# Output projection, layer normalisation and gate logits merged into one stage, with the gate weights stationary in four column groups and one softmax over all tokens

## The chip, the cores and the metric

The kernel is one program on one core of a Trainium2 chip. The metric is the device time of one execution in microseconds (us). The core has five engines that run their own queues and meet only through semaphores: TensorE (PE), VectorE (DVE), ScalarE (ACT), GpSimd (POOL) and SyncE (SP); transfers are issued from the queues of SP, ACT and POOL.

## The reference

The whole function is two transformer-like layers on x of 8 x 1024 x 256 in float32: attention, a routed mixture of experts, a phase attention and a soft mixture of experts, each on a normalised input. The change concerns this part of the first layer:

```python
# end of the attention: ctx is 8 x 1024 x 256
x  = x + ctx @ Wo + bo
xn = (x - mean(x)) / sqrt(var(x) + 1e-5)           # over the 256 features
logits   = einsum('bsd,de->bse', xn, gate_w)       # 8 experts
affinity = softmax(logits, axis=-1)
gating, index = top_k(transpose(affinity), 256)    # per batch and expert, of 1024 tokens
```

The chosen rows of xn then go through their expert, are weighted by gating, and are added to x.

## The kernel before

The program is a row of stages. Each stage (class Stage) has its own tiles and semaphores, begins with a barrier of all engines, and hands its results to the next stage through device memory (DRAM). A token tile is 128 tokens in 128 partitions; there are 64 of them. Three stages and a search stand between the attention (attend) and the experts:

- **project** (pj_ names): 16 turns of four token tiles (512 tokens). SP loads the attention's output, already transposed (ctxT, tile pj_c), and the residual x (tile pj_x), four turns ahead. POOL adds the bias to x (L866), PE multiplies ctx with Wo (L842: per turn four tiles by two halves of the 256 features), DVE adds the two (L859), and ACT's queue stores x1 (L850). No engine waits in one turn for another turn's tail, except through the four buffers.
- **normalise** (n_ names, called three more times elsewhere): eight turns of 1024 tokens. DVE takes mean and variance (L149, L154), ACT the square root (L199), DVE reciprocal, scales (L166, L167) and the normalised xn (L175), PE transposes it (L191), ACT copies that out of PSUM (L217), and ACT's queue stores xn (L211) and xnT (L222).
- **route** (rt_ names): eight turns of one batch. SP loads xnT, PE multiplies with the tokens as the weights and the 256 x 8 gate matrix as the moving operand (L942), DVE and ACT compute a softmax per batch (L967 to L974, exponential L959). Then PE turns the affinities so that each of 128 partitions holds 512 tokens of one batch and expert (L947), and DVE searches: 32 rounds of max, max_index and match_replace (L990 to L992), after which the sorted halves are merged and the weights and indices stored.

An engine executes its instructions strictly in the order in which they are written; a wait blocks all that is behind it on that engine.

Of the kernel before, what the change touches and what calls it, by code (L numbers as in the profile page):

```python
# [9 lines left out]
ALU = mybir.AluOpType  # L10
# [3 lines left out]
P = 128  # L14
# [777 lines left out]
def project(nc, tag, ctxT_d, w_d, b_d, x_d, out_d):  # L792

    TC = 4
    TURNS = TILES // TC
    N = TC * P
    U = 4
    rows = lambda d, t: d[t * N:(t + 1) * N, :].rearrange("(t p) d -> p t d", p=P)
    with Stage(nc, tag) as st:
        w = st.sb("w", [P, KD, D])  # L800
        bias = st.sb("bias", [P, D])
        c = [st.sb(f"c{j}", [P, KD, N]) for j in range(U)]
        x = [st.sb(f"x{j}", [P, TC, D]) for j in range(U)]
        mm = [st.ps(f"mm{j}", [P, TC, D]) for j in range(4)]
        w_in = st.sem("w_in")
        bias_in = st.sem("bias_in")
        ctx_in = [st.sem(f"ctx_in{j}") for j in range(U)]
        x_in = [st.sem(f"x_in{j}") for j in range(U)]
        biased = st.sem("biased")
        made = st.sem("made")  # L810
        summed = st.sem("summed")
        stored = [st.sem(f"stored{j}") for j in range(U)]
        with st.block() as block:

            @block.sync
            def _(sp):
                def loads(t):

                    j, b, t0 = t % U, t // 2, t % 2 * N
                    if t >= U:  # L820
                        sp.wait_ge(made, FLOOR + t - U + 1)
                    sp.dma_start(c[j][:], ctxT_d[b, :, t0:t0 + N].rearrange("(k p) t -> p k t", p=P)).then_inc(ctx_in[j], 16)
                    if t >= U:
                        sp.wait_ge(stored[j], FLOOR + 16 * (t // U))
                    sp.dma_start(x[j][:], rows(x_d, t)).then_inc(x_in[j], 16)

                sp.dma_start(w[:], w_d.rearrange("(k p) n -> p k n", p=P)).then_inc(w_in, 16)
                loads(0)
                sp.dma_start(bias[:], col_bcast(b_d)).then_inc(bias_in, 16)
                for t in range(1, TURNS):  # L830
                    loads(t)

            @block.tensor
            def _(pe):
                pe.wait_ge(w_in, FLOOR + 16)
                for t in range(TURNS):
                    pe.wait_ge(ctx_in[t % U], FLOOR + 16 * (t // U + 1))
                    if t >= 4:
                        pe.wait_ge(summed, FLOOR + t - 3)
                    for q in range(TC):  # L840
                        for k in range(KD):
                            ins = pe.matmul(mm[t % 4][:, q, :], c[t % U][:, k, q * P:(q + 1) * P], w[:, k, :],  # L842
                                            start=k == 0, stop=k == KD - 1)
                    ins.then_inc(made, 1)

            @block.scalar
            def _(act):
                for t in range(TURNS):
                    act.wait_ge(summed, FLOOR + t + 1)
                    act.dma_start(rows(out_d, t), x[t % U][:]).then_inc(stored[t % U], 16)  # L850
                for j in range(U):
                    act.wait_ge(stored[j], FLOOR + 16 * TURNS // U)

            @block.vector
            def _(dve):
                for t in range(TURNS):
                    dve.wait_ge(biased, FLOOR + t + 1)
                    dve.wait_ge(made, FLOOR + t + 1)
                    dve.tensor_tensor(x[t % U][:], x[t % U][:], mm[t % 4][:], ALU.add).then_inc(summed, 1)  # L859

            @block.gpsimd
            def _(pool):
                pool.wait_ge(bias_in, FLOOR + 16)
                for t in range(TURNS):
                    pool.wait_ge(x_in[t % U], FLOOR + 16 * (t // U + 1))
                    pool.tensor_tensor(x[t % U][:], x[t % U][:],  # L866
                                       bias[:].rearrange("p (a n) -> p a n", a=1).broadcast_to([P, TC, D]),
                                       ALU.add).then_inc(biased, 1)


def route(nc, xnT_d, gate_d, ident_d, rowbase_d, idx_d, wt_d):


    U = 4
# [3 lines left out]
    with Stage(nc, "rt") as st:  # L878
        ident = st.sb("ident", [P, P])
        rowbase = st.sb("rowbase", [P, 1])  # L880
        gw = st.sb("gw", [P, KD, E])
        xT = [st.sb(f"xT{u}", [P, KD, T]) for u in range(U)]
        lg = st.sb("lg", [P, NT, E])
        ex = st.sb("ex", [P, NT, E])
        mx = st.sb("mx", [P, NT])
        sm = st.sb("sm", [P, NT])
# [11 lines left out]
        lp = [st.ps(f"lp{j}", [P, NT, E]) for j in range(2)]  # L898
        rows = st.ps("rows", [P, HALF])
        cols = st.ps("cols", [P, 2, 2, P])  # L900
        c_in = st.sem("c_in")
        x_in = [st.sem(f"x_in{u}") for u in range(U)]
        made = st.sem("made")
        read = st.sem("read")
# [4 lines left out]
        turned = st.sem("turned")  # L909
# [4 lines left out]
        with st.block() as block:  # L914

            @block.sync
            def _(sp):
                sp.dma_start(ident[:], ident_d).then_inc(c_in, 16)
                sp.dma_start(rowbase[:], rowbase_d).then_inc(c_in, 16)
                sp.dma_start(gw[:], gate_d.rearrange("(k p) e -> p k e", p=P)).then_inc(c_in, 16)  # L920
                for b in range(B):

                    if b >= U:
                        sp.wait_ge(made, FLOOR + (b - U + 1))
                    sp.dma_start(xT[b % U][:], xnT_d[:, :, b * T:(b + 1) * T].rearrange("k p t -> p k t")
                                 ).then_inc(x_in[b % U], 16)
                sp.wait_ge(chosen, FLOOR + 2)
                sp.dma_start(wt_d, wt[:]).then_inc(stored, 16)
                sp.dma_start(idx_d, idx[:]).then_inc(stored, 16)
                sp.wait_ge(stored, FLOOR + 32)  # L930

            @block.tensor
            def _(pe):
                pe.wait_ge(c_in, FLOOR + 48)
                with pe.Fori(0, B // U) as i:
                    for u in range(U):
                        j = u % 2
                        pe.wait_ge(x_in[u], FLOOR + (i * 16 + 16))
                        pe.wait_ge(read, FLOOR + (i * U + max(u - 1, 0)))
                        for t in range(NT):  # L940
                            for k in range(KD):
                                ins = pe.matmul(lp[j][:, t, :], xT[u][:, k, t * P:(t + 1) * P], gw[:, k, :],  # L942
                                                start=k == 0, stop=k == KD - 1)
                        ins.then_inc(made, 1)
                pe.wait_ge(aff_ready, FLOOR + 1)
                for t in range(TT):
                    ins = pe.transpose(rows[:, t * P:(t + 1) * P], aff[:, t].rearrange("p h n -> p (h n)"), ident[:])  # L947
                ins.then_inc(turned, 1)
                pe.wait_ge(both_ready, FLOOR + 2)
                for q in range(2):  # L950
                    for s in range(2):
                        ins = pe.transpose(cols[:, q, s, :], both[:, q, s * P:(s + 1) * P], ident[:])
                ins.then_inc(turned_back, 1)

            @block.scalar
            def _(act):
                with act.Fori(0, B) as b:
                    act.wait_ge(shifted, FLOOR + (b + 1))
                    act.activation(ex[:], lg[:], ACT.Exp).then_inc(exped, 1)  # L959

            @block.vector
            def _(dve):
                for b in range(B):
                    j = b % 2
                    ch = Chain(dve, chain, b, 4)
                    dve.wait_ge(made, FLOOR + (b + 1))
                    ch.link(dve.tensor_reduce(mx[:], lp[j][:], AX.X, ALU.max))  # L967
                    dve.tensor_tensor(lg[:], lp[j][:], mx[:].rearrange("p (t a) -> p t a", a=1).broadcast_to([P, NT, E]),
                                      ALU.subtract).then_inc(shifted, 1)
                    dve.wait_ge(shifted, FLOOR + (b + 1))  # L970
                    dve.wait_ge(exped, FLOOR + (b + 1))
                    ch.link(dve.tensor_reduce(sm[:], ex[:], AX.X, ALU.add))
                    ch.link(dve.reciprocal(sm[:], sm[:]))
                    ch.link(dve.tensor_tensor(  # L974
                        aff[:, :, :, b * E:(b + 1) * E].rearrange("p t h e -> p h t e"),
# [1140 lines left out]
```

## Time and profile before

| | |
|---|---|
| time before, median of three runs | 5498.03 us (5489.18 to 5511.64) |
| the profiled execution's own time | 5504.3 us |
| its span in the profile | 5502.5 us |
| PE, DVE, ACT, POOL busy in the span | 87%, 60%, 38%, 22% |
| mean granted TensorE clock | 0.917 |
| project: first transfer issued at 1895.14 us; normalise: 1976.34 us; route: 2055.71 us; first expert's matrices multiplied from 2214.20 us | |

The shares of busy time are averages over all stages. Since a barrier stands between the stages, the time of a stage is that from its first transfer's issue to the next stage's, and what bounds one stage says nothing of another.

### The profile page before, as it was taken

The numbers are of one execution on the slowest core, as the hardware profiler recorded it, in microseconds if no ns is written. First come the engines' busy times: TensorE is split into PE (matmuls) and PEld (weight loads), VectorE is DVE, ScalarE is ACT, GpSimd is POOL, SyncE is SP. The second block draws the span as 40 slices with busy tenths as digits, with TensorE's granted clock in tenths as the row PEclk, the third lists the DMA queues.
The fourth block names the chain that finished last, engine by engine and source line by source line (L and its number), as shares of the span: only waits on it lengthen the run. The fifth ranks groups of instructions, "written<-read, shape, count | busy, mean of one in ns | idle before, by whom it ended". The sixth has DMA issues, their size and how long they took to land. (4 is left out here: it accounts for less than half of the span.)

```text
span 5502.5 us, 72404 instructions
## 1 busy us (share of the span) xinstructions
PE 4772.4 (87%) x28132; PEld 3134.7 (57%) x28132; DVE 3328.4 (60%) x3921; ACT 2107.9 (38%) x3437; POOL 1207.2 (22%) x864
## 2 busy tenths in 40 slices
PE   5879999999999654999993867774899999979999
PEld 3512222222222243788883434333899999978888
DVE  5578888888888145111114687775677677744443
ACT  1037777777677310222221433332222222223333
POOL 1432222211221110444440101010233233310000
PEclk9979999999999865999995888785999999999999
DMA  6543344444433491333326101016744455454553
GB/s 215 182 68 57 60 80 73 76 69 84 75 59 56 121 322 48 86 61 70 73 45 231 48 31 61 30 61 218 201 97 97 97 112 99 97 147 169 181 181 132
DMA packets 479632, 587.57 MB, mean 107 GB/s; under 512 B 32176, under 2 KB 393904, under 8 KB 470960
## 3 DMA queue, kind: packets, MB, share of 16 engines
q1 hardware_dynamic: 261424, 391.61, 27.7%
q10 hardware_dynamic: 193408, 159.40, 11.8%
q0 software_dynamic: 24576, 33.57, 3.8%
q8 instruction: 140, 2.29, 0.2%
q14 instruction: 84, 0.69, 0.0%
HBM read 306.47 MB, written 227.67 MB: 97 GB/s over the span
## 5 line engine op out<-in xcount | busy, mean ns | idle before, releaser
L743 DVE TENSOR_REDUCE att_nmx<-att_s 128x1 f32<-128x1024 f32 x1024 | 1204.9, 1219 | 231.9 <-PE att_s L653 228.6
L729 ACT ACTIVATE att_pt<-att_sT 128x512 f32<-128x512 f32 x2048 | 1058.9, 604 | 471.1 <-PE att_sT L670 470.6
L653 PE MATMUL att_s<-att_KT,att_QT 96*128 96x512 bf16 x2048 | 790.6, 390 | 48.0 <-DMA att_KT<-att_hi 38.0
L670 PE MATMUL att_sT<-att_QT,att_KT 128*128 128x512 bf16 x2048 | 778.9, 383 | 6.1 <-ACT att_pt L729 6.1
L670 PEld LDWEIGHTS att_sT<-att_QT,att_KT 128*128 128x128 bf16 x2048 | 197.6, 97 | 650.6 <-ACT att_pt L729 459.2
L684 PE MATMUL att_o<-att_pt,att_va 128*32 128x512 f32 x4096 | 553.6, 607 | 0.0
L1744 PE MATMUL sl_lp<-sl_phi,sl_xT 128*128 (+1 forms) x4160 | 492.4, 277 | 31.7 <-DMA sl_xT<-xnT 23.2
L1733 POOL TENSOR_TENSOR sl_lg<-sl_lg,sl_sm 128x512 f32<-128x512 f32 x256 | 319.6, 1269 | 880.7 <-DVE sl_sm L1871 880.7
L1744 PEld LDWEIGHTS sl_lp<-sl_phi,sl_xT 128*128 128x128 f32 x4160 | 479.9, 194 | 38.6 <-issue 38.6
L1984 PE MATMUL cb_op<-cb_y,cb_exT 128*128 128x256 f32 x2048 | 485.4, 380 | 0.0
L1782 PE MATMUL sl_acc<-sl_lg,sl_xn 128*128 128x128 f32 x4096 | 478.3, 275 | 0.0
L1782 PEld LDWEIGHTS sl_acc<-sl_lg,sl_xn 128*128 128x128 f32 x4096 | 467.7, 192 | 0.0
L1199 DVE TENSOR_TENSOR moe_hT<-moe_sg,moe_up 128x512 f32<-128x512 f32 x128 | 88.0, 688 | 620.3 <-PE moe_yp L1136 356.6
L1804 ACT ACTIVATE sl_lg<-sl_lg 128x1024 f32<-128x1024 f32 x128 | 135.3, 1057 | 763.4 <-DVE sl_lg L1860 763.4
L1984 PEld LDWEIGHTS cb_op<-cb_y,cb_exT 128*128 128x128 f32 x2048 | 370.6, 191 | 40.2
L653 PEld LDWEIGHTS att_s<-att_KT,att_QT 96*128 96x128 bf16 x2048 | 198.7, 99 | 245.0 <-DVE att_nmx L743 49.8
L1869 DVE TENSOR_REDUCE sl_sm<-sl_lg 128x128 f32<-128x1024 f32 x128 | 248.7, 1943 | 136.5 <-ACT sl_lg L1804 136.5
L191 PE MATMUL n_tr<-n_ident,n_xn 128*128 128x128 f32 x512 | 125.9, 427 | 193.2 <-DVE n_xn L175 148.9
L1086 POOL DMA_INDIRECT x<-moe_y,moe_idx x128 | 204.3, 1596 | 339.4 <-ACT moe_y L1176 319.9
L579 POOL COPY att_QT<-att_QT 32x1024 bf16<-32x1024 bf16 x64 | 72.5, 1159 | 921.6 <-DVE att_QT L764 921.3
L1122 PE MATMUL moe_gp<-moe_xT,moe_wg 128*128 128x256 f32 x1024 | 243.9, 381 | 0.8 <-ACT moe_xT L1161 0.8
L1122 PE MATMUL moe_up<-moe_xT,moe_wu 128*128 128x256 f32 x1024 | 243.1, 380 | 0.0
(206 smaller groups left out, 6341.0 us busy)
## 6 DMA issues: line engine op xcount, KB each, us to landing
lg<-sl_raw ACTq DMA_DIRECT2D x128, 512.0 KB
cb_ex<-lg SPq DMA_DIRECT2D x64, 1024.0 KB, 8.3
xnT<-n_xnT ACTq DMA_DIRECT2D x64, 512.0 KB, 5.6
n_x<-x SPq DMA_DIRECT2D x27, 1024.0 KB, 9.1
xn<-n_xn ACTq DMA_DIRECT2D x24, 1024.0 KB, 9.4
sl_w<-in_L_ffn_W SPq DMA_DIRECT2D x68, 256.0 KB
qk<-qkv_turned ACTq DMA_DIRECT2D x64, 256.0 KB, 3.3
att_qin<-qk SPq DMA_DIRECT2D x64, 256.0 KB
```

The source lines that it names most:

```text
L653: ins = pe.matmul(s[i % 2][:, c, :], QT[n % NB][0:ROWS, h, t * P:(t + 1) * P], KT[n % NB][0:ROWS, h, c * 512:(c + 1) * 512], start=True, s ...
L670: pe.matmul(sT[:, idx % 3, :], KT[g % NB][:, h, kt * P:(kt + 1) * P], QT[g % NB][:, h, step // 4 * 512:(step // 4 + 1) * 512], start=True, ...
L684: ins = pe.matmul(o[32 * h:32 * h + 32, :], va[g % 2][:, kt, h, :], pt[:, step % 2, h, c, :], start=kt == 0, stop=kt == NT - 1)
L729: act.activation(pt[:, step % 2, h, c, :], sT[:, idx % 3, :], ACT.Exp, scale=HD ** -0.5).then_inc(exp_done, 1)
L743: dve.tensor_reduce(nmx[n % 2][:, t, h:h + 1], s[i % 2][:].rearrange("p c k -> p (c k)"), AX.X, ALU.max, negate=True).then_inc(freed, 1)
L1086: pool.indirect_dma_start(x_d, bass.IndirectOffsetOnAxis(idx[:, s, column(n):column(n) + 1], 0), y[n % NY][:, s, :], None, compute_op=ALU. ...
L1122: ins = pe.matmul(o_[:, m, :], w_[:, k, (2 * h + m) * P:(2 * h + m + 1) * P], xT[n % 2][:, k, :], start=k == 0, stop=k == KD - 1)
L1733: pool.tensor_tensor(part_, part_, sm[j][:].rearrange("p (a n) -> p a n", a=1).broadcast_to([P, HB, P]), ALU.mult).then_inc(shared, 1)
L1744: ins = pe.matmul(lp[j][:, b, :], xT[:, k, b * T + m * P:b * T + (m + 1) * P], ph[:, k, bass.ds(c * P, P)], start=k == 0, stop=k == KD - 1)
L1782: ins = pe.matmul(acc[:, k, b, :], xn[:, b * NT + m, k * P:(k + 1) * P], lg[m % 4][:, b, :], start=m == 0 and b % 4 == 0, stop=m == NT - 1 ...
L1869: ch.link(dve.tensor_reduce(sm[j][:], lg[l][:].rearrange("p b n -> p n b"), AX.X, ALU.add))
L1984: ins = pe.matmul(op[n % 2][:], exT[n % 2][:, s, :], y[b % 2][:, s, :], start=s == 0, stop=s == SK - 1)
```

## The change

The three calls project, normalise and route become one stage, project_route, with 16 turns of 512 tokens. The residual sum stays in SBUF and is normalised there; the transposed xn stays in SBUF too and is neither stored nor loaded; x1 and xn are still stored, for the experts. xn is now computed by ACT (four activations with scale and bias from tiles), not by DVE. One copy of 128 x 1024 takes a turn's transposes out of PSUM. For the gate logits the operands swap: the gate matrix, filled up with zeros to 32 columns, is the weights, and 128 transposed tokens are the moving operand; the four token tiles of a turn go to four groups of 32 output partitions (gl). ACT copies the 128 x 128 result to SBUF, PE turns it back (gT), and DVE takes the 8 useful columns of each 32 into lg. After the last turn there is one softmax over all 64 tiles; the turn into rows, the search and the merge are as before.

PE, ACT and DVE each run a hand-written order of turns that lag behind each other:

```diff
-    project(nc, "pj", ctxT, a["L0_attn_Wo"], a["L0_attn_bo"], x0, x1)
-    normalise(nc, "n1", x1, xn, xnT, ident)
-    route(nc, xnT, a["L0_ffn_gate_w"], ident, a["rowbase"], idx, wt)
+    project_route(nc, ctxT, a["L0_attn_Wo"], a["L0_attn_bo"], x0, a["L0_ffn_gate_w"], ident, a["rowbase"], x1, xn, idx, wt)
...
+    U, UX = 4, 6
+    EW = 32
...
+        mm = [st.ps(f"mm{j}", [P, TC, D]) for j in range(2)]
+        tr = st.ps("tr", [P, KD, N])
+        gl = st.ps("gl", [P, 512])
+        gT = st.ps("gT", [P, 512])
...
+                def loads(t):
...
+                    if t >= U:
+                        sp.wait_ge(made, FLOOR + t - U + 1)
+                    sp.dma_start(c[t % U][:], ctxT_d[b, :, t0:t0 + N].rearrange("(k p) t -> p k t", p=P)
+                                 ).then_inc(ctx_in[t % U], 16)
+                    if t >= UX:
+                        sp.wait_ge(x_stored[t % UX], FLOOR + 16 * (t // UX))
+                        sp.wait_ge(xn_ready, FLOOR + t - UX + 1)
+                    sp.dma_start(x[t % UX][:], rows_of(x_d, t)).then_inc(x_in[t % UX], 16)
...
             @block.tensor
             def _(pe):
...
+                def output(t):
...
+                    pe.wait_ge(ctx_in[t % U], FLOOR + 16 * (t // U + 1))
+                    if t >= 2:
+                        pe.wait_ge(summed, FLOOR + t - 1)
+                    for q in range(TC):
+                        for k in range(KD):
+                            ins = pe.matmul(mm[t % 2][:, q, :], c[t % U][:, k, q * P:(q + 1) * P], w[:, k, :],
+                                            start=k == 0, stop=k == KD - 1)
+                    ins.then_inc(made, 1)
...
+                def turn(t):
...
+                    pe.wait_ge(xn_ready, FLOOR + t + 1)
+                    if t >= 1:
+                        pe.wait_ge(xnT_ready, FLOOR + t)
+                    for k in range(KD):
+                        for q in range(TC):
+                            ins = pe.transpose(tr[:, k, q * P:(q + 1) * P], xn[t % 3][:, q, k * P:(k + 1) * P], ident[:])
+                    ins.then_inc(turned, 1)
...
+                def gate(t):
...
+                    pe.wait_ge(xnT_ready, FLOOR + t + 1)
+                    if t >= 1:
+                        pe.wait_ge(gls_ready, FLOOR + t)
+                    for k in range(KD):
+                        for q in range(TC):
+                            ins = pe.matmul(gl[q * EW:(q + 1) * EW, 0:P], gw[:, k, :], xnT[t % 2][:, k, q * P:(q + 1) * P],
+                                            start=k == 0, stop=k == KD - 1)
+                    ins.then_inc(gated, 1)
...
+                def turn_gate(t):
...
+                    pe.wait_ge(gls_ready, FLOOR + t + 1)
...
+                    pe.transpose(gT[:, 0:P], gls[t % 2][:], ident[:]).then_inc(g_turned, 1)
...
+                for t in range(TURNS + 3):
+                    if t < TURNS:
+                        output(t)
...
+                    if 0 <= t - 1 < TURNS:
+                        turn(t - 1)
+                    if 0 <= t - 2 < TURNS:
+                        gate(t - 2)
+                    if 0 <= t - 3 < TURNS:
+                        turn_gate(t - 3)
...
             @block.scalar
             def _(act):
...
+                def deviation(t):
...
+                    act.wait_ge(var_ready, FLOOR + t + 1)
...
+                    act.activation(rstd[t % 2][:], mv[t % 2][:, :, 1], ACT.Sqrt, bias=eps[:, 0:1]).then_inc(dev_ready, 1)
+                    act.dma_start(rows_of(x1_d, t), x[t % UX][:]).then_inc(x_stored[t % UX], 16)
...
+                def normal(t):
...
+                    act.wait_ge(nmr_ready, FLOOR + t + 1)
...
+                    for q in range(TC):
+                        ins = act.activation(xn[t % 3][:, q, :], x[t % UX][:, q, :], ACT.Identity,
+                                             bias=nmr[t % 2][:, q:q + 1], scale=rstd[t % 2][:, q:q + 1])
+                    ins.then_inc(xn_ready, 1)
+                    act.wait_ge(xn_ready, FLOOR + t + 1)
+                    act.dma_start(rows_of(xn_d, t), xn[t % 3][:]).then_inc(xn_stored[t % 3], 16)
...
+                def take_turned(t):
...
+                    act.wait_ge(turned, FLOOR + t + 1)
...
+                    act.activation(xnT[t % 2][:], tr[:], ACT.Copy).then_inc(xnT_ready, 1)
...
+                def take_gate(t):
...
+                    act.wait_ge(gated, FLOOR + t + 1)
...
+                    act.activation(gls[t % 2][:], gl[:, 0:P], ACT.Copy).then_inc(gls_ready, 1)
...
+                for t in range(TURNS + 3):
+                    if t < TURNS:
+                        deviation(t)
+                    if 0 <= t - 1 < TURNS:
+                        normal(t - 1)
+                    if 0 <= t - 2 < TURNS:
+                        take_turned(t - 2)
+                    if 0 <= t - 3 < TURNS:
+                        take_gate(t - 3)
+                act.wait_ge(shifted, FLOOR + 1)
+                act.activation(lg[:], lg[:], ACT.Exp).then_inc(exped, 1)
...
             @block.vector
             def _(dve):
...
+                def add(t):
...
+                    dve.wait_ge(biased, FLOOR + t + 1)
+                    dve.wait_ge(made, FLOOR + t + 1)
+                    dve.tensor_tensor(x[t % UX][:], x[t % UX][:], mm[t % 2][:], ALU.add).then_inc(summed, 1)
...
+                for t in range(TURNS + 4):
+                    if t < TURNS:
+                        add(t)
+                        statistics(t)
+                    if 0 <= t - 1 < TURNS:
+                        scales(t - 1)
+                    if 0 <= t - 4 < TURNS:
+                        take(t - 4)
```

statistics(t) is four bn_stats of 128 x 256 and four bn_aggr with a wait between them, scales(t) a reciprocal and one operation of 128 x 4, take(t) a copy of 128 x 32. POOL's bias addition is that of before.

## Rows read from the trace of the kernel before

**Rows 1.** The page, the chain that ended last, by line.

```profile
PE cb_op L1984 8%; PE cb_tr L1970 2%; DMA cb_ex<-lg 0%; DVE cb_nmx L2030 0%; ACT cb_ex L2005 0%; ACT cb_exT L2013 0%; DVE cb_x L2048 0%; SPq L1939 0%; SPq L1930 0%; SPq L1924 0%; DVEq L2047 0%
```

**Rows 2.** Windows of the three stages: length, busy (count) of each engine, clock, DMA share, GB/s.

```profile
1895.00:1976.00 81.00, 61.10 (x256) 49.87 (x256) 19.54 (x16) 0.00 (x0) 37.52 (x16) 0.90 0.92 316
1976.00:2055.00 79.00, 31.47 (x128) 25.11 (x128) 53.13 (x225) 21.36 (x42) 0.00 (x0) 0.50 0.94 333
2055.00:2120.50 65.50, 54.95 (x256) 54.76 (x256) 8.72 (x40) 12.31 (x16) 0.00 (x0) 0.50 0.36 130
```

**Rows 3.** Groups by line and shape, 1880 to 2210 us: count, busy us, mean ns, idle before.

```profile
L866 POOL TENSOR_TENSOR pj_x<-pj_x,pj_bias 128x1024 f32<-128x1024 f32 x16 | 37.5, 2345 | 43.3 <-DMA pj_x<-in_x 28.8 <-DMA pj_bias<-in_L_attn_bo 14.5
...
L859 DVE TENSOR_TENSOR pj_x<-pj_x,pj_mm 128x1024 f32<-128x1024 f32 x16 | 19.5, 1221 | 84.0 <-PE pj_mm L842 46.4 <-POOL pj_x L866 37.6
...
L959 ACT ACT_TABLE_LOAD x8 | 10.3, 1283 | 6.9 <-PEq L74 6.6
...
L199 ACT ACT_TABLE_LOAD x1 | 1.3, 1283 | 126.6 <-DVE n_mv L154 126.6
```

**Rows 4.** Timeline of project: start, length in us, engine, line, operation, count.

```profile
1895.14 0.38 SPq L827 DMA_DIRECT2D pj_w<-in_L_attn_Wo  x1
...
1900.04 20.54 PE L842 MATMUL pj_mm<-pj_w,pj_c 128*128 128x256 f32 x80 [41.82 <-DMA pj_c<-ctxT]
...
1906.87 1.22 DVE L859 TENSOR_TENSOR pj_x<-pj_x,pj_mm 128x1024 f32<-128x1024 f32 x1 [39.69 <-PE pj_mm L842]
...
1951.10 3.72 PE L842 MATMUL pj_mm<-pj_w,pj_c 128*128 128x256 f32 x16 [1.89 <-DMA pj_c<-ctxT]
```

**Rows 5.** Timeline of normalise.

```profile
1985.47 2.71 DVE L149 BATCH_NORM_STATS2 n_stats<-n_x 128x6 f32<-128x256 f32 x8
...
1995.03 0.64 DVE L154 BATCH_NORM_AGGREGATE n_mv<-n_stats 128x2 f32<-128x6 f32 x8
...
1995.55 1.97 PE L191 MATMUL n_tr<-n_ident,n_xn 128*128 128x128 f32 x8 [1.18 <-ACT n_xnT L217]
...
1997.55 1.09 ACT L217 ACTIVATE n_xnT<-n_tr 128x512 f32<-128x512 f32 x2 [2.06 <-PE n_tr L191]
...
1998.88 0.88 ACTq L222 DMA_DIRECT2D xnT<-n_xnT  x2
...
2000.33 0.47 ACTq L211 DMA_DIRECT2D xn<-n_xn  x1
2000.92 1.09 ACT L217 ACTIVATE n_xnT<-n_tr 128x512 f32<-128x512 f32 x2 [0.74 <-PE n_tr L191]
...
2022.26 0.30 ACT L199 ACTIVATE n_rstd<-n_mv,n_eps 128x8 f32<-128x8 f32 x1 [2.22 <-DVE n_xn L175]
2022.48 0.41 ACTq L211 DMA_DIRECT2D xn<-n_xn  x1
```

**Rows 6.** Timeline at the end of route's softmax.

```profile
2120.32 0.23 DVE L974 TENSOR_TENSOR rt_aff<-rt_ex,rt_sm 128x64 f32<-128x64 f32 x1
```

**Rows 7.** Timeline of the last stage's start, PE alone.

```profile
4934.10 3.45 PE L1970 MATMUL cb_tr<-cb_ident,cb_ex 128*128 128x128 f32 x16 [22.55 <-ACT cb_ex L2005]
```

**Rows 8.** Windows of 1 us with the granted clock (third from the end).

```profile
1906.00:1907.00 1.00, 1.00 (x5) 0.83 (x5) 0.13 (x1) 0.00 (x0) 0.07 (x1) 0.91 1.07 386
...
4937.00:4938.00 1.00, 0.55 (x4) 0.30 (x2) 0.00 (x0) 0.00 (x0) 0.00 (x0) 0.89 0.99 410
...
4940.00:4941.00 1.00, 0.00 (x0) 0.00 (x0) 0.79 (x2) 0.46 (x1) 0.00 (x0) 0.81 1.04 434
```

**Rows 9.** Timeline of the attention, PE alone.

```profile
1000.69 1.06 PE L684 MATMUL att_o<-att_pt,att_va 128*32 128x512 f32 x8
1001.69 0.39 PE L670 MATMUL att_sT<-att_QT,att_KT 128*128 128x512 bf16 x1
```

**Rows 10.** Timeline of the experts, ACT alone.

```profile
2307.29 0.84 ACT L1176 ACTIVATE moe_y<-moe_yp,moe_wt 128x256 f32<-128x256 f32 x2 [2.86 <-PE moe_yp L1136]
```

**Rows 11.** Groups by line and shape, whole span.

```profile
L1808 ACT ACTIVATE sl_raw<-sl_lp 128x1024 f32<-128x1024 f32 x128 | 128.7, 1006 | 0.0
```

More of the change, by code:

```diff
@@ L796, in project @@
     N = TC * P
[L797 to L868, printed above, removed]
@@ L871, in route @@
-def route(nc, xnT_d, gate_d, ident_d, rowbase_d, idx_d, wt_d):
-    U = 4
+    U, UX = 4, 6
+    EW = 32
     TT = NT // 2
@@ L877, in route @@
     R = B * E
-    with Stage(nc, "rt") as st:
+    rows_of = lambda d, t: d[t * N:(t + 1) * N, :].rearrange("(t p) d -> p t d", p=P)
+    with Stage(nc, "pr") as st:
         ident = st.sb("ident", [P, P])
         rowbase = st.sb("rowbase", [P, 1])
[L881 to L886, printed above, removed]
+        w = st.sb("w", [P, KD, D])
+        bias = st.sb("bias", [P, D])
+        gw = st.sb("gw", [P, KD, EW])
+        eps = st.sb("eps", [P, 1])
+        c = [st.sb(f"c{j}", [P, KD, N]) for j in range(U)]
+        x = [st.sb(f"x{j}", [P, TC, D]) for j in range(UX)]
+        stats = st.sb("stats", [P, TC, 6])
+        mv = [st.sb(f"mv{j}", [P, TC, 2]) for j in range(2)]
+        rstd = [st.sb(f"rstd{j}", [P, TC]) for j in range(2)]
+        nmr = [st.sb(f"nmr{j}", [P, TC]) for j in range(2)]
+        xn = [st.sb(f"xn{j}", [P, TC, D]) for j in range(3)]
+        xnT = [st.sb(f"xnT{j}", [P, KD, N]) for j in range(2)]
+        gls = [st.sb(f"gls{j}", [P, P]) for j in range(2)]
+        lg = st.sb("lg", [P, TILES, E])
+        mx = st.sb("mx", [P, TILES])
+        sm = st.sb("sm", [P, TILES])
         aff = st.sb("aff", [P, TT, 2, R])
@@ L930, in _ @@
                 sp.wait_ge(stored, FLOOR + 32)
+            @block.gpsimd
+            def _(pool):
+                pool.memset(gw[:], 0.0).then_inc(cleared, 1)
+                pool.memset(eps[:], LN_EPS).then_inc(eps_ready, 1)
+                pool.wait_ge(bias_in, FLOOR + 16)
+                for t in range(TURNS):
+                    pool.wait_ge(x_in[t % UX], FLOOR + 16 * (t // UX + 1))
+                    pool.tensor_tensor(x[t % UX][:], x[t % UX][:],
+                                       bias[:].rearrange("p (a n) -> p a n", a=1).broadcast_to([P, TC, D]),
+                                       ALU.add).then_inc(biased, 1)
@@ L961, in _ @@
+                for j in range(UX):
+                    act.wait_ge(x_stored[j], FLOOR + 16 * len(range(j, TURNS, UX)))
+                for j in range(3):
+                    act.wait_ge(xn_stored[j], FLOOR + 16 * len(range(j, TURNS, 3)))
             @block.vector
             def _(dve):
[L963 to L975, printed above, removed]
-                        ex[:].rearrange("p (h t) e -> p h t e", h=2),
-                        sm[:].rearrange("p (h t a) -> p h t a", h=2, a=1).broadcast_to([P, 2, TT, E]),
-                        ALU.mult))
-                    ch.close()
-                    dve.sem_inc(read, 1)
@@ L981, in _, with statistics @@
-                dve.sem_inc(aff_ready, 1)
-                ch = Chain(dve, chain)
-                ch.base = 4 * B
-                dve.wait_ge(turned, FLOOR + 1)
-                ch.link(dve.tensor_copy(work[:], rows[:]))
+                def add(t):
+                    dve.wait_ge(biased, FLOOR + t + 1)
+                    dve.wait_ge(made, FLOOR + t + 1)
+                    dve.tensor_tensor(x[t % UX][:], x[t % UX][:], mm[t % 2][:], ALU.add).then_inc(summed, 1)
+                def statistics(t):
+                    dve.wait_ge(summed, FLOOR + t + 1)
+                    if t >= 1:
+                        dve.wait_ge(var_ready, FLOOR + t)
+                    for q in range(TC):
+                        ins = dve.bn_stats(stats[:, q, :], x[t % UX][:, q, :])
+                    ins.then_inc(stats_ready, 1)
+                    dve.wait_ge(stats_ready, FLOOR + t + 1)
+                    if t >= 2:
+                        dve.wait_ge(nmr_ready, FLOOR + t - 1)
+                    for q in range(TC):
+                        ins = dve.bn_aggr(mv[t % 2][:, q, :], stats[:, q, :])
+                    ins.then_inc(var_ready, 1)
@@ new lines, in _ @@
+                wide = lambda v: v[:].rearrange("p (t a) -> p t a", a=1).broadcast_to([P, TILES, E])
+                ch = Chain(dve, chain)
+                dve.wait_ge(taken, FLOOR + TURNS)
+                ch.link(dve.tensor_reduce(mx[:], lg[:], AX.X, ALU.max))
+                dve.tensor_tensor(lg[:], lg[:], wide(mx), ALU.subtract).then_inc(shifted, 1)
+                dve.wait_ge(exped, FLOOR + 1)
+                ch.link(dve.tensor_reduce(sm[:], lg[:], AX.X, ALU.add))
+                ch.link(dve.reciprocal(sm[:], sm[:]))
@@ new lines, in _ @@
+                for h in range(2):
+                    ins = dve.tensor_tensor(
+                        aff[:, :, h, :].rearrange("p t (b e) -> p b t e", e=E),
+                        lg[:].rearrange("p (b h t) e -> p h b t e", h=2, t=TT)[:, h],
+                        sm[:].rearrange("p (b h t a) -> p h b t a", h=2, t=TT, a=1)[:, h].broadcast_to([P, B, TT, E]),
+                        ALU.mult)
+                ins.then_inc(aff_ready, 1)
+                dve.wait_ge(rows_ready, FLOOR + 1)
@@ L988, in _ @@
+                rows = mm[0][:, 0:2, :].rearrange("p t d -> p (t d)")
+                cols = mm[1][:, 0:2, :].rearrange("p t d -> p (t d)").rearrange("p (q s n) -> p q s n", q=2, s=2)
+                ch.link(dve.tensor_copy(work[:], rows))
                 for r in range(CAP // 8):
```

93 lines of the change are left out of this document (64 added, 29 removed).

## Prediction

> **What bounds the kernel now.** I began with the page's chain of waits. It names only the last stage [rows 1], because a barrier stands before each stage; it says nothing of the changed ones. What counts for them is how long they last, and the windows by stage show it [rows 2]. From project's first transfer at 1895.14 us [rows 4] to the last affinity of route's softmax at 2120.32 + 0.23 = 2120.55 us [rows 6] it is 225.4 us. The reader should see three different limits. In project the DMA share is 0.92: transfers bound it, and PE runs at a granted clock of 0.90. In normalise transfers again (0.94), PE at 0.50. In route PE is busy for 54.95 of 65.50 us at 0.50, with 8-column matmuls that wait for their weight loads. The search behind it is not changed; its time cancels. So the question is what replaces these 225.4 us.
>
> **What goes.** The load of x1, the store and the load of xnT (8.4 MB each: 64 tiles of 128 x 256 x 4 bytes), two barriers, 128 xn operations on DVE, 128 of route's PE products with 128 weight columns, and seven of eight softmax turns with their exponential-table loads of 1.28 us [rows 3]. Left are ctx, x, x1 and xn, 2.1 MB a turn. At normalise's 333 GB/s [rows 2] that is 6.3 us a turn, 101 us in all. If transfers still set the pace, this would be a large gain. They don't, by the order of the queues.
>
> **What comes: a ring through four engines.** Follow turn t in the loops. PE runs output(t), turn(t-1), gate(t-2), turn_gate(t-3). turn(t-1) waits for normal(t-1), which stands on ACT behind deviation(t), and that waits for DVE's statistics of turn t, which need output(t). turn(t-1) also waits for take_turned(t-2), which empties the only tr buffer and stands on ACT behind normal(t-1). And output(t+1) stands on PE behind turn_gate(t-3). So the turns don't overlap: while DVE and ACT work, PE has nothing it may do. Behind the waiting turn(t-1) are queued gate, turn_gate and the next output, and DVE waits for that. Two mm buffers and four loads ahead do not help. One turn costs the sum around the ring:
>
> 1. DVE from the last matmul on: add 1.22 [rows 3]; four bn_stats, half of 2.71 plus the pipe's end, 1.43; four bn_aggr, from 0.64 for eight, 0.37 [rows 5]; three handovers, 0.24 by the gaps of such rows. 3.26 us.
> 2. ACT: the square root, and the x1 store's issue 0.22 us behind its start (2022.48 less 2022.26), 0.38 to 0.47 long, then 0.12 to the next operation (2000.33 + 0.47 to 2000.92) [rows 5]: 0.72. Four normalising activations of 128 x 256: two with one operand from a tile take 0.84 [rows 10], so four take 1.6; these have two such operands, and I take 1.75 (bounds 1.6 and 2.1). ACT waits for its own end and issues xn's store: 0.24 (1997.55 + 1.09 to 1998.88) plus issue and gap [rows 5], 0.7. The copy of 128 x 1024 out of PSUM: 1.0 [rows 11]. Sum 4.2 us (3.9 to 4.6).
> 3. PE: eight transposes at the low clock 1.8 (1.97 with the last one's drain [rows 5]). The gate products: four column groups in float32 with 512 columns take 1.00 us to the next start at the full clock [rows 9]; 128 columns are a quarter, twice for the halves of 256 features, 0.5 at full and 0.9 at the low clock. turn_gate 0.25. Changes of tile shape and handovers 0.2. Sum 3.15 us.
> 4. The output product: 6.83 us at the low clock (1900.04 to 1906.87), 3.43 at full (20.54 less 6.83, over four) [rows 4].
>
> The price of the shape change: the column groups' row shows 1.00 us where 512 columns in four passes at 2.4 GHz stream for 0.85, so about 0.15 a turn [rows 9]. The Trainium skill, TensorEngine Tiling (Array Packing), Key Properties, says that changing the tiling mode drains TensorE; the trace agrees with a small drain, and that rule against this change is worth about 2 us in 16 turns. On the activations, the Trainium skill, ScalarE: Activation LUTs, What ACT_TABLE_LOAD costs, gives 93 ns for each operand from a tile; by it the four would take about 2.1 us, an estimate from that page that would add some 5 us in all; no row of before has two such operands.
>
> The clock decides the fourth term. PE idles over 7 us a turn in steps 1 and 2. In the last stage PE stopped at 4937.55 [rows 7] and the clock fell at about 4940.6 [rows 8], 3.1 us later, so here it falls in every turn to 1.2 GHz. It came back 3.1 us after a dense start (4934.10 to 4937.2, transposes alone [rows 7, 8]) and 6.2 us after another (1900.04 to 1906.2 [rows 4, 8]). Counted from the transposes, 2.95 us before the output, the output then takes 3.5 to 5.0 us; counted from the output's own start, if the gate products are too thin, 5.0 to 6.5. I take 5.3, slightly above the middle. The ring is 3.26 + 4.2 + 3.15 + 5.3 = 15.9 us. That DVE loses xn and PE loses the slow gate products doesn't shorten it, because none of them overlaps with anything now.
>
> **The sum**, from the first transfer. output(0) starts at 4.9 [rows 4], ends at 11.7, output(1) follows at full clock to 15.2. DVE 3.3, root and normal(0) 2.4, transposes 1.8: output(2) starts at 22.7. Thirteen rings of 15.9 later output(15) starts at 229.4 and ends at 234.7. Tail: DVE and ACT 7.5, take_gate 0.3, normal(15) and store 2.5, copy 1.0, transposes 2.0, copy 1.0, gate 1.1, take_gate 0.3, turn back 0.5, take 0.2: 16.4. One softmax on 128 x 512: two reductions and a subtraction at 0.65 (half of 1.22 [rows 3]), exponential 0.6, reciprocal 0.5, two products 0.6, handovers: 4.3. About 31 more semaphores to set at the stage's start, 1. End: 256.4 us. ACT loads tables once for the root, since normalise alternates root and copies with a single load [rows 3], and the one for the exponential lies beside PE's last steps. POOL's 2.35 us [rows 3] and 2.1 MB of transfers lie inside a ring of 15.9 us and cost nothing; without that cover transfers would be 6.3. The last stores lie beside the search.
>
> 256.4 - 225.4 = +31.0 us. Against its own time: 5504.3 becomes 5535. The median of the runs shown, 5498.0, is 0.1% below that execution; from it, 5529 us, +0.56%.
>
> **The rivals.** Half a per cent, 27.5 us, is about what a measurement of this kernel can tell from no change.
>
> *The clock is back before the output* (chance 0.25). Then a ring is 14.1 to 14.9, so 1.4 less than mine in 14 rings, 20 us: +11 us, 5509. For it: transposes alone brought it back once [rows 7, 8].
>
> *The clock holds through the idle time* (0.1). Output 3.5, transposes and gate 1.2 less: ring 12.9, -8 us, 5490. Against it: the fall after 3.1 idle us [rows 8].
>
> *The ring doesn't exist, and transfers set the pace* (0.07): the other side. Decided if turn(t-1) could pass ahead of output(t)'s statistics; from a ring below 11.6 it is faster by over 0.5%. 4.9 + 16 x 6.3 + 16.4 + 4.3 + 1 = 127 us, -98, about 5400. For it stand only the DMA shares [rows 2]; the orders in the code speak against it.
>
> *The column groups don't overlap, or the clock stays low throughout* (0.13). Eight products one after the other at 0.43 add 2.5 to each ring: +35 on mine, 5564. A low output of 6.83 adds 1.5: +21, 5550.
>
> *That it does what I sum* (0.45), own range 5520 to 5545: the activations, and the clock's return, decide inside it.
>
> **How the numbers follow.** Slower by over 0.5%: most of the forecast case (0.40) and the last rival (0.13), 0.53. Within 0.5%: the early clock (0.25), the rest of the forecast (0.05), most of the clock that holds (0.09): 0.39. Faster: 0.08. The range of 8 in 10 leaves out the transfer case and the extreme ends: 5497 to 5560.
>
> **What would show it.** In the profile after: output products start every 15 to 17 us, not every 6; PE idle some 7.5 us before each turn's transposes, released by ACT's xn; the granted clock of the stage between 0.5 and 0.8; DMA share near 0.4; about 256 us to the last affinity; the search unchanged. A stage with DMA share over 0.9 would prove the ring wrong; output products of 3.5 us, the clock step; ACT's four activations over 2.1 us or a table load in each turn, step 2.

## The result, and the profile after

The changed kernel takes 5526.7 us (median of 10 runs, 5519.4 to 5533.7), the kernel before 5500.6 us (10 runs, 5489.2 to 5512.0). The ratio is 1.0041 with a 95% interval of 1.0029 to 1.0052: 0.4% slower. Forecast were 5529 us, +0.56%, in a range of 5497 to 5560. The size lies just inside the half per cent that I had called indistinguishable from no change; the direction is certain.

The window from the stage's first transfer to the last affinity (columns: length, busy us and count of PE, PEld, DVE, ACT, POOL, granted clock, DMA share, GB/s):

```profile
1907.16:2149.11 241.95, 119.01 (x656) 92.32 (x656) 57.71 (x198) 60.20 (x115) 37.68 (x18) 0.73 0.43 141
```

It is 241.95 us against the 225.4 of the three stages before, which [rows 2] show in three parts; forecast were 255.4, and 1 us for the start. The DMA share of 0.43 stands where 0.92 and 0.94 stood. PE is busy for half the time only. Before this window lies a second loss: from attention's last store to the merged stage's first transfer it is 9.15 us (timeline of the changed kernel),

```profile
1898.01 0.38 SPq L523 DMA_DIRECT2D ctxT<-att_num  x1
1907.16 0.38 SPq L890 DMA_DIRECT2D pr_w<-in_L_attn_Wo  x1
```

where in the trace before it was 6.4 (up to project's first transfer at 1895.14 us):

```profile
1888.72 0.38 SPq L523 DMA_DIRECT2D ctxT<-att_num  x1
```

Up to the experts' first transfer the changed stages take 323.1 us (1907.16 to 2230.23) against 306.5 (1895.14 to 2201.61): 16.6 more, and 2.7 in the gap, 19.3 us together. The other 2.1 of the 21.4 us between the two profiled spans are in stages with the same code: attention came out 8.5 us longer, the phase attention 9.6 shorter. Over all the traces of this study, attention takes 1626 to 1636 us up to the next stage's first transfer (less the 2.7 us where there are more semaphores) and the phase attention 746 to 762, so this is spread and not the change. The ratio gives 23 us, with 16 to 29 inside the interval, which 19.3 fits.

One turn of the ring, in the timeline of the changed kernel (start, length in us, engine, line, operation, and in brackets the idle time before it and what ended it):

```profile
1965.94 1.22 DVE L1041 TENSOR_TENSOR pr_x<-pr_x,pr_mm 128x1024 f32<-128x1024 f32 x1 [11.02 <-PE pr_mm L925]
...
1967.20 1.41 DVE L1049 BATCH_NORM_STATS2 pr_stats<-pr_x 128x6 f32<-128x256 f32 x4
1968.64 0.38 DVE L1055 BATCH_NORM_AGGREGATE pr_mv<-pr_stats 128x2 f32<-128x6 f32 x4
...
1969.05 0.30 ACT L988 ACTIVATE pr_rstd<-pr_mv,pr_eps 128x4 f32<-128x4 f32 x1 [10.20 <-DVE pr_mv L1055]
...
1969.56 2.07 ACT L998 ACTIVATE pr_xn<-pr_x,pr_nmr,pr_rstd 128x256 f32<-128x256 f32 x4 [0.21 <-issue]
...
1971.66 0.38 ACTq L1002 DMA_DIRECT2D xn<-pr_xn  x1
1972.14 1.02 ACT L1009 ACTIVATE pr_xnT<-pr_tr 128x1024 f32<-128x1024 f32 x1 [0.51 <-ACT pr_xn L998]
1973.07 0.27 ACT L1016 ACTIVATE pr_gls<-pr_gl 128x128 f32<-128x128 f32 x1
...
1973.31 1.94 PE L936 MATMUL pr_tr<-pr_ident,pr_xn 128*128 128x128 f32 x8 [7.48 <-ACT pr_xnT L1009]
...
1975.18 1.08 PE L946 MATMUL pr_gl<-pr_xnT,pr_gw 128*32 128x128 f32 x16
...
1976.20 0.48 PE L955 MATMUL pr_gT<-pr_ident,pr_gls 128*128 128x128 f32 x1
...
1976.46 5.13 PE L925 MATMUL pr_mm<-pr_w,pr_c 128*128 128x256 f32 x16
...
1981.70 1.22 DVE L1041 TENSOR_TENSOR pr_x<-pr_x,pr_mm 128x1024 f32<-128x1024 f32 x1 [12.32 <-PE pr_mm L925]
```

The reader should follow the starts downward: each operation begins when the one above it ends, and no two engines do much at once. DVE adds and takes statistics (1965.94 to 1969.0), ACT takes the root, normalises, issues the store, copies (to 1973.2), PE transposes and multiplies (to 1981.6), and DVE begins again at 1981.70. PE waits 7.48 us before its transposes. The waits of the stage, summed, say it too (who waited for whom: us, times, longest):

```profile
DVE pr_x L1041 <- PE pr_mm L925: 201.4, 16, 42.6
ACT pr_rstd L988 <- DVE pr_mv L1055: 150.1, 15, 11.5
POOL pr_x L912 <- DMA pr_x<-in_x: 126.0, 15, 14.0
...
PE pr_tr L936 <- ACT pr_xnT L1009: 105.1, 15, 7.8
```

The transposes' wait of 105.1 us is put down to ACT's copy out of PSUM (pr_xnT), which came last, and not to xn, as the forecast's list of signs had it; both waits are in its ring. POOL waits for x only because SP may not reload a buffer sooner; these transfers are late by the ring and do not set it. Three groups by line and shape:

```profile
L998 ACT ACTIVATE pr_xn<-pr_x,pr_nmr,pr_rstd 128x256 f32<-128x256 f32 x64 | 33.2, 589 | 3.3 <-issue 2.5 <-DVE pr_nmr L1065 0.5
...
L946 PE MATMUL pr_gl<-pr_xnT,pr_gw 128*32 128x128 f32 x256 | 16.5, 404 | 0.5 <-ACT pr_gls L1016 0.5
...
L988 ACT ACT_TABLE_LOAD x1 | 1.3, 1283 | 54.1 <-DVE pr_mv L1055 54.1
```

ACT's four normalising activations take 2.07 us, not 1.75. Each has two operands from tiles and starts 0.49 us behind the one before (2.07 less 0.59, over three). Here the Trainium skill's figure (ScalarE: Activation LUTs, What ACT_TABLE_LOAD costs), by which I had estimated 2.1, was nearer than my value. There is one table load for the root in the whole stage. The gate's 16 records of a turn take 1.08 us at the low clock; one after the other, at the forecast's price of 0.43 us for each of eight products, they would take 3.4. So the column groups do overlap.

### The profile page after: what moved, and what is told of

Read it like the earlier page. It is cut to its first block and busy times, and to the rows that moved or that the text cites. A ratio compares the mean times of both kernels' runs of the same rounds, so it can differ in the third digit from the quotient of the medians.

```text
span 5523.9 us, 72227 instructions
## 1 busy us (share of the span) xinstructions
PE 4736.7 (86%) x28148; PEld 3091.2 (56%) x28148; DVE 3310.1 (60%) x3838; ACT 2135.1 (39%) x3494; POOL 1209.9 (22%) x866
## 5 line engine op out<-in xcount | busy, mean ns | idle before, releaser
L1251 PE MATMUL moe_yp<-moe_wd,moe_hT 128*128 128x256 f32 x1024 | 231.6, 379 | 1.4 <-DVE moe_hT L1314 1.4
```

What stands on the lines that cost most here:

```text
L1251: ins = pe.matmul(yp[n % 2][:, s, :], hT[m // 2][:, m % 2, s * P:(s + 1) * P], wd[j][:, m, :], start=m == 0, stop=m == NI - 1)
```

## The experiments

Kernels that were timed in rounds are compared with the kernel before on the same chip. "Turn" is the mean distance of DVE's additions from the third on: 14.84 us in the changed kernel (1936.68 to 2129.63 in 13 turns). Only e9 leaves a part of the computation out.

**e1: ACT's order alone.** deviation(t) goes last.

```diff
+                    if 0 <= t - 1 < TURNS:
+                        normal(t - 1)
...
                     if 0 <= t - 3 < TURNS:
                         take_gate(t - 3)
+                    if t < TURNS:
+                        deviation(t)
```

> ACT alone gets another order in a turn: normal(t-1), take_turned(t-2), take_gate(t-3), and deviation(t) last. DVE and PE keep theirs. Ring theory (a turn costs the sum around PE, DVE, ACT): normal(t-1) still waits for scales(t-1), which stands on DVE behind statistics(t) and so behind output(t). Only the square root and the x1 store's issue leave the ring, 0.4 us a turn, and scales' 0.3 us comes in: output products start every 14.7 to 15.1 us, the time stays within 0.2% of the changed kernel's. Rival (it was ACT's order alone that held PE back, or transfers or one engine's own work set the pace): the turns draw together to below 10 us and the time falls by over 50 us.

Measured: 5521.5 us, 1.0032 (1.0019 to 1.0046); turn 14.47 us, 0.37 less, and so a little below the 14.7 to 15.1 expected. The turns did not draw together to below 10 us: it is not ACT's order alone.

**e2: ACT's and DVE's order.** On DVE scales(t-1) and take(t-4) come before add(t) and statistics(t), on top of e1.

```diff
+                    if 0 <= t - 1 < TURNS:
+                        scales(t - 1)
+                    if 0 <= t - 4 < TURNS:
+                        take(t - 4)
                     if t < TURNS:
                         add(t)
                         statistics(t)
```

> As the run before, and DVE's order too: scales(t-1), take(t-4), then add(t) and statistics(t). No work is added or removed. Ring theory: output(t) is then beside the work of turn t-1 on ACT and DVE; from the end of output(t-1) it is some 8.3 us to turn(t-1), and that and the next output products share a period of two turns of 13.5 us at the full clock, 16.7 at the low one: a turn of 6.7 to 8.4 us, transfers at 6.3 not far below, stage 130 to 150 us, total time 5410 to 5440 us, about 1.5% under the kernel before. Rival (the transfers or an engine's own work fill the turn of 15 us): no change of over 10 us.

Measured: 5421.7 us, 0.9837 (0.9810 to 0.9865); turn 6.79 us; last affinity 133.1 us after the first transfer (1905.11 to 2038.2). With the same instructions the turn falls to less than half. The work was never 15 us a turn; the order of two queues was. In its timeline the output product (1976.84) now runs beside ACT and DVE:

```profile
1975.10 1.06 PE L936 MATMUL pr_tr<-pr_ident,pr_xn 128*128 128x128 f32 x8 [0.37 <-ACT pr_xnT L1009]
...
1976.84 3.62 PE L925 MATMUL pr_mm<-pr_w,pr_c 128*128 128x256 f32 x16
...
1980.56 1.22 DVE L1041 TENSOR_TENSOR pr_x<-pr_x,pr_mm 128x1024 f32<-128x1024 f32 x1 [1.81 <-PE pr_mm L925]
...
1982.51 1.06 PE L936 MATMUL pr_tr<-pr_ident,pr_xn 128*128 128x128 f32 x8 [2.06 <-ACT pr_xnT L1009]
...
1983.35 2.36 POOL L912 TENSOR_TENSOR pr_x<-pr_x,pr_bias 128x1024 f32<-128x1024 f32 x1 [5.35 <-DMA pr_x<-in_x]
...
1984.21 1.51 DVE L1065 SCALAR_TENSOR_TENSOR pr_nmr<-pr_mv,pr_rstd 128x4 f32<-128x4 f32 x1
1984.25 3.62 PE L925 MATMUL pr_mm<-pr_w,pr_c 128*128 128x256 f32 x16
```

The last but one of these rows is a finding of its own, below.

**e3: the idle time filled.** The changed kernel's orders, and 14 products that nothing reads.

```diff
                     ins.then_inc(made, 1)
+                    if 1 <= t:
+                        pe.wait_ge(summed, FLOOR + t)
+                        for i in range(14):
+                            pe.matmul(mm[(t + 1) % 2][:, 0, :], w[:, 0, 0:P], w[:, 0, :], start=True, stop=True)
```

> The changed kernel with 14 extra float32 products of 256 columns after each output product from turn 1 on; they write a PSUM tile that the next output product overwrites, and serve only to keep PE busy for 6.0 of the 7.4 us in which it waited. Clock theory (the idle time costs PE the full clock, in all 2 to 3 us a turn): granted clock of the stage 1.0, output product 3.5 to 3.7 us, transposes 1.0, gate products 0.6; ring 12.9 us instead of 15.0, total time 25 to 30 us below the changed kernel, so even with the kernel before. Rival (the clock costs little, handovers and the other engines' terms make the ring): less than 8 us gained; or, if the extra products meet the low clock and take 12 us, slower by up to 5 us a turn.

Measured: 5500.5 us, 0.9992 (0.9980 to 1.0003), 26 us under the changed kernel; turn 12.83 us against 12.9 expected. PE in its timeline:

```profile
2007.59 1.06 PE L940 MATMUL pr_tr<-pr_ident,pr_xn 128*128 128x128 f32 x8 [1.44 <-ACT pr_xnT L1013]
2008.58 0.65 PE L950 MATMUL pr_gl<-pr_xnT,pr_gw 128*32 128x128 f32 x16
2009.16 0.33 PE L959 MATMUL pr_gT<-pr_ident,pr_gls 128*128 128x128 f32 x1
2009.32 3.62 PE L925 MATMUL pr_mm<-pr_w,pr_c 128*128 128x256 f32 x16
2012.78 6.21 PE L931 MATMUL pr_mm<-pr_w 128*128 128x256 f32 x28
2020.42 1.06 PE L940 MATMUL pr_tr<-pr_ident,pr_xn 128*128 128x128 f32 x8 [1.44 <-ACT pr_xnT L1013]
```

Windows of the turns in the middle, first the changed kernel's, then this one's:

```profile
1937.00:2115.00 178.00, 88.57 (x491) 68.63 (x491) 39.47 (x143) 42.59 (x83) 23.43 (x10) 0.73 0.40 130
```

```profile
1927.00:2090.00 163.00, 144.30 (x881) 121.06 (x880) 39.86 (x143) 45.66 (x89) 23.45 (x10) 1.00 0.44 144
```

More work on PE made the kernel faster, by as much as it had lost: the granted clock goes from 0.73 to 1.00, the transposes from 1.94 to 1.06 us, the gate products from 1.08 to 0.65, the output product to 3.6.

**e4: 31 spare semaphores** in project of the kernel before, never waited on.

```diff
+        spare = [st.sem(f"spare{j}") for j in range(31)]
```

> The kernel before with 31 more semaphores allocated in project, never waited on. The changed kernel's merged stage has 49 semaphores against project's 18, and its first transfer came 9.15 us after attention's last store was issued, against 6.42. If the semaphores make that gap: it becomes 9.0 to 9.3 us here as well. If it was something else (the transfer's landing, the memsets): it stays at 6.4 to 6.6.

Measured: one run, 5506.3 us; what counts is the gap in its timeline, 9.12 us:

```profile
1887.26 0.38 SPq L523 DMA_DIRECT2D ctxT<-att_num  x1
1896.38 0.38 SPq L828 DMA_DIRECT2D pj_w<-in_L_attn_Wo  x1
```

So 2.7 us of the loss are the merged stage's 49 semaphores against 18, 87 ns for each one more on average (2.70 / 31).

**e5: PE's order alone**, in the changed kernel.

```diff
-                for t in range(TURNS + 3):
-                    if t < TURNS:
-                        output(t)
+                for t in range(-1, TURNS + 3):
+                    if t + 1 < TURNS:
+                        output(t + 1)
```

> The changed kernel with only PE's order altered: output(t+1), turn(t-1), gate(t-2), turn_gate(t-3) in a turn, so that the output product runs one turn ahead of before; ACT and DVE keep their order. Ring theory: the ring can be cut at any one of its links. output(t+1) is then done before ACT and DVE need it, PE works beside them, and a turn falls to the longest of PE's own 5.4 us at the full clock, ACT's 5.4 us and the transfers' 6.3: output products every 6.3 to 7.5 us, total time 5405 to 5430 us, like the run with ACT's and DVE's order altered. Rival (only the place of the root and the statistics matters): stays above 5490 us.

Measured: 5416.1 us, 0.9823 (0.9799 to 0.9846); last affinity 136.1 us after the start. One cut at another link does the same: the next output product now stands on PE ahead of the transposes that wait for ACT. Turns come in pairs of 5.2 and 7.7 to 11.6 us; their mean of 7.4 is at the upper end of what was expected.

**e6: both cuts**, e2 and e5 together.

> Both cuts together: PE one turn ahead, and ACT's and DVE's statistics last. In the run with one cut the stage took 133 us to the last affinity at a DMA share of 0.87 to 0.97 in its first 100 us. If transfers are the limit there: no more than 5 us less than the better single cut. If waits of the ring were still the limit: 10 to 20 us less.

Measured: 5391.5 us, 0.9783 (0.9762 to 0.9804); every turn from the sixth on 5.16 us; last affinity 107.2 us after the start. The stage is 26 us shorter than in e2 and 29 shorter than in e5, more than the 10 to 20 expected if waits were still the limit, and not the 5 at most if transfers were. I had leaned to the transfers as e2's limit, but waits made up this difference; which of them did was not tried. PE's timeline has no gap left,

```profile
1953.23 3.62 PE L925 MATMUL pr_mm<-pr_w,pr_c 128*128 128x256 f32 x16
1956.69 1.04 PE L936 MATMUL pr_tr<-pr_ident,pr_xn 128*128 128x128 f32 x8
1957.65 0.64 PE L946 MATMUL pr_gl<-pr_xnT,pr_gw 128*32 128x128 f32 x16
1958.23 0.33 PE L955 MATMUL pr_gT<-pr_ident,pr_gls 128*128 128x128 f32 x1
1958.39 3.62 PE L925 MATMUL pr_mm<-pr_w,pr_c 128*128 128x256 f32 x16
```

and its windows show PE busy throughout, at the full clock, at 389 GB/s:

```profile
1945.00:1965.00 20.00, 20.00 (x163) 16.77 (x162) 13.15 (x47) 13.74 (x28) 7.07 (x3) 1.00 1.08 389
1965.00:1985.00 20.00, 20.00 (x163) 16.75 (x162) 13.13 (x49) 14.00 (x28) 9.42 (x4) 1.00 1.08 389
```

**e10: which of the two bounds e6?** Two more products in each turn.

```diff
+                    for i in range(2):
+                        pe.matmul(tr[:, 0, 0:D], w[:, 0, 0:P], w[:, 0, :], start=True, stop=True)
                     for k in range(KD):
```

> Both cuts, and two more float32 products of 256 columns on PE in each turn, 0.86 us at the full clock; they are overwritten by the transposes. With both cuts a turn took 5.16 us at a PE busy share of 1.0 and 389 GB/s. If PE sets that pace: 6.0 us a turn. If the transfers set it: PE's extra work is taken up and a turn stays within 5.2 to 5.5 us.

Measured: one run, 5408.4 us; turns of 6.02 and 6.03 us, 0.86 more, exactly the added work. PE bounds e6, and the transfers of 2.1 MB fit into its 5.16 us: 406 GB/s by that division, 389 by the windows, against the 333 by which I had called 6.3 us their floor.

**e7 to e9: DVE's small operation.** L1065 takes 0.16 us, but 1.51 in e2's rows above, where it ends with POOL's bias addition (1984.21 + 1.51 = 1985.72; 1983.35 + 2.36 = 1985.71). e7 is e2 with two plain products in its place:

```diff
-                    dve.scalar_tensor_tensor(nmr[t % 2][:], mv[t % 2][:, :, 0], -1.0, rstd[t % 2][:], ALU.mult, ALU.mult
-                                             ).then_inc(nmr_ready, 1)
+                    dve.tensor_tensor(nmr[t % 2][:], mv[t % 2][:, :, 0], neg[:], ALU.mult).then_inc(neg_ready, 1)
...
+                    dve.tensor_tensor(nmr[t % 2][:], nmr[t % 2][:], rstd[t % 2][:], ALU.mult).then_inc(nmr_ready, 1)
```

> The run with ACT's and DVE's order altered, in which DVE's operation L1065 of 128 x 4 took 0.16 us in most turns but up to 2.34, each time until POOL's bias addition ended. Here it is replaced by two plain tensor_tensor products of 128 x 4, one with a tile of -1. If it is that form of instruction that waits for POOL: none of the new ones takes over 0.3 us, and a turn loses some of ACT's wait for it (12.9 us in the whole stage), total time 0 to 10 us less. If any DVE operation of SBUF operands waits for POOL: the same long ones appear.

Measured: 5423.3 us, 0.9843 (0.9824 to 0.9863), no gain. The wait had moved to the first of the plain products. e8 is e6 with the same edit.

> Both cuts and the two plain products together. If transfers set the pace by then, the same time as both cuts alone, within 5 us; if ACT's wait behind POOL was still in the ring, up to 10 us less.

Measured: 5404.1 us, 0.9801 (0.9777 to 0.9825), no gain either: the stage took 111.9 us to the last affinity against e6's 107.2, and the first of the plain products again took up to 2.17 us. e9 is e2 without POOL's addition; the bias is left out of the sum.

```diff
-                    pool.tensor_tensor(x[t % UX][:], x[t % UX][:],
...
-                    dve.wait_ge(biased, FLOOR + t + 1)
+                    dve.wait_ge(x_in[t % UX], FLOOR + 16 * (t // UX + 1))
```

> The run with ACT's and DVE's order altered, without POOL's addition of the output bias (left out of the computation). There DVE's small operation L1065, which reads two tiles of SBUF, took up to 2.34 us, ending with POOL's. If DVE and POOL exclude each other on such operations: all 16 of L1065 take 0.16 to 0.17 us. If something else stretched them (the semaphores, the root on ACT): the long ones stay. The output product's turns stay in the band of 5.2 to 9.3 us, because transfers still take 2.1 MB a turn.

Measured: one run, 5422.6 us. The instructions on nmr in e2, e7 and e9, in this order (durations in ns: least, median, most; first and last start):

```profile
L1065 DVE SCALAR_TENSOR_TENSOR pr_nmr<-pr_mv,pr_rstd x16: 161/164/2339, 1922.2 to 2024.9; 128x4 f32<-128x4 f32 x16
```

```profile
L1069 DVE TENSOR_TENSOR pr_nmr<-pr_mv,pr_neg x16: 130/132/1711, 1918.7 to 2024.3; 128x4 f32<-128x4 f32 x16
L1072 DVE TENSOR_TENSOR pr_nmr<-pr_nmr,pr_rstd x16: 161/163/165, 1919.5 to 2024.6; 128x4 f32<-128x4 f32 x16
```

```profile
L1060 DVE SCALAR_TENSOR_TENSOR pr_nmr<-pr_mv,pr_rstd x16: 161/162/164, 1920.3 to 2020.7; 128x4 f32<-128x4 f32 x16
```

Without POOL's work none is long. In e2 five of the 16 took over 0.17 us, and each of the five ended within 0.03 us of an addition on POOL. In e7 it was the instruction before, not the form, that waited.

## Why the prediction was right, step by step

**The ring** held. e1, e2 and e5 settle it: it opens when one link is cut (turns of 7.4 us and less), and does not when ACT's order alone moves the root away. The transfer rival (5400 us) was excluded by the order of the queues, as argued. Once the order allowed it, the time fell even below that rival's (e6, 5391.5), but there PE sets the pace and not the transfers (e10).

**Its terms.** DVE: 1965.94 to 1969.05 is 3.11 us, against 3.26: a handover inside the engine costs 0.03. ACT: 1969.05 to the copy's end at 1973.16 is 4.11, against 4.2. The activations cost 0.3 us more, and the rest less: the x1 store's issue starts with the root (0.01 us behind it, not 0.22), so the first activation comes 0.51 us after it, not 0.72, and ACT's wait for its own end is 0.03, not 0.24. PE: from the transposes at 1973.31 to the output product at 1976.46 is 3.15 us, as forecast, in parts of 1.87, 1.02 and 0.26.

**The clock**, the mis-sized term. It fell in each idle time: from output(3) on all transposes take 1.94 us, the low clock. It came back within most output products, and in three of the 13 turns before the product began: from output(3) on the products take 3.6 to 5.1 us, and the turns differ by just that (14.15 to 15.76 us). The mean turn of 14.84 less 3.11, 4.11, 0.15 for the handover to PE and 3.15 leaves 4.3 us for the output product, against 5.3. I had weighed two countings, from the transposes (3.5 to 5.0) and from the output (5.0 to 6.5), and taken the middle. The profile fits the first. One turn of the changed kernel shows it directly, in a window with the granted clock third from the end:

```profile
2003.93 1.94 PE L936 MATMUL pr_tr<-pr_ident,pr_xn 128*128 128x128 f32 x8 [7.48 <-ACT pr_xnT L1009]
...
2006.98 3.62 PE L925 MATMUL pr_mm<-pr_w,pr_c 128*128 128x256 f32 x16
```

```profile
2006.00:2007.00 1.00, 1.00 (x18) 0.58 (x12) 0.00 (x0) 0.00 (x0) 0.00 (x0) 0.59 0.00 0
```

A mean of 0.59 over this microsecond, between 0.50 and 1.00, puts the return at about 2006.8 us, before the output product's start at 2006.98. Since its last idle time PE had run only transposes, gate products and the turn back. The term mis-sized is nearly the whole error: thirteen turns from output(2) to output(15) took 194.7 us (1930.81 to 2125.52) against 206.7. e3 shows the price of the clock as such: 2.0 us a turn, against 3.0 between my ring of 15.9 and that of a held clock.

**The semaphores** I had priced at 1 us, a figure that no row showed; they cost 2.7 (e4).

**The tail.** From the last output product's end (2129.5) to the last affinity it is 19.6 us; forecast were 16.4 and 4.3. The softmax is 4.2 us of them, with the exponential's table load beside PE's last steps, as said.

**The agreement of the totals is in part luck.** Thirteen rings were forecast 12.0 us too long, the last output product 1.3 and the tail 1.1; the start was 1.0 too short (the first output product began 6.2 us after the first transfer, not 4.9) and the semaphores 1.7. So +31.0 becomes the +19.3 that the stages' own lengths show. That the median of all runs lies only 2 us from 5529 owes the rest to the spread of the other stages and of the runs. Of the three outcomes, slower by over half a per cent had the highest chance (0.53), and the measured 0.41% fell just into the next (0.39). Of the signs named, the turns of 15 to 17 us and the 256 us came out shorter (14.84 and 242); PE's idle 7.5 us, the granted clock, the DMA share and the 2.1 us for the activations held.

**What I had wrong beside the path:** the transfers' floor of 6.3 us a turn, taken from normalise's mean rate. It touched only a rival's price and e2's and e6's expectations. By its length the ring lies at the edge of the rival with the early clock (14.1 to 14.9), and in three of 13 turns the clock was back before the output, as that rival says. In the other ten it returned inside the output product, which is the forecast case, whose own range of 5520 to 5545 holds the time. The stages' +19.3 us lie between that rival's +11 and the forecast's +31.

So where did the saved work go? 25 MB of transfers, seven softmaxes and PE's slow gate products were removed, and transfers and gate products had been the limits of their stages. But the new stage is not bound by the work that is left (5.16 us a turn in e6); it is bound by the order in which three queues hand it round.

The version that beats both kernels is e6: 5391.5 us, 2.2% under the kernel before.

## What to carry to other kernels

When several lagged steps are written into the same turn on each queue, follow one turn's dependences through every queue before counting work: if the step that waits for this turn's product stands ahead of the step that feeds the next turn on another engine, the engines take turns however many buffers there are. Let one engine run ahead, or put what waits for this turn last on each queue; either cut shortened the stage by 106 to 109 us here. An idle PE also costs its clock on return, here 2 us a turn.

## What the runs showed of the hardware that I had not expected

Two forms of DVE operation with both operands in SBUF (L1065 in e2, its plain product in e7) stood still while POOL ran its addition on SBUF. A 128 x 4 operation of 0.16 us took up to 2.34, ending with POOL's 2.36 us addition, and 0.16 in all 16 turns when POOL had nothing to do (e9). DVE's addition with one operand in PSUM (1206 to 1223 ns), the bn_stats (407 to 430) and the reciprocal (177 to 179) kept their times in e2 beside POOL. The Trainium skill states this (SBUF — State Buffer, section SBUF: two separate sides: the pair of ports that DVE and GpSimd share is an exclusive lock, which a DVE operation with two SBUF inputs needs when the GpSimd operation reads SBUF), and the runs agree. It was worth some four microseconds of stage time: up to the experts' first transfer 210.2 us in e9 against 214.2 in e2, by one trace of each.

The 31 semaphores more cost 87 ns each on average before a stage could start (e4). The price is not even: e7 and e8 have one more than the changed kernel, and their gap is 9.36 us against 9.13 to 9.15 in the others with the merged stage. And stages whose code is the same in all kernels spread by 10 to 16 us from one execution to the next, so one pair of profiles can't settle a difference of that size; the stage's own length could.
